# A gated transformer and Mamba kernel whose loop bodies list the same calls in another order

## The reference

```python
def attn_layer(x, Wqkv, qs, ksc, Wo):
    q, k, v = heads(x @ Wqkv)                       # 16 heads of 64
    q, k = rotary(l2norm(q) * qs), rotary(l2norm(k) * ksc)
    out = local_attention(q, k, v)                  # each window of 32 sees 64 keys
    return out @ Wo
def ffn_layer(x, g, bln, W1, b1, W2, b2):
    a, gate = split((layernorm(x) * g + bln) @ W1 + b1)
    return a * gelu(gate) @ W2 + b2
for i in range(6):
    x = attn_layer(shift_tokens(x), ...) + x
    x = ffn_layer(shift_tokens(x), ...) + x
# Mamba: conv -> silu -> delta, B, C;  h_t = exp(delta A) h_{t-1} + delta B x;  y = sum_n h C
x = x + s * silu(g)
```

## Time and profile before

| what | value |
|---|---|
| runs (3) | 1778.52 us median, 1778.05 to 1781.15 |
| profiled execution: span, first to last instruction | 1776.2 us |
| profiled execution: own time | not listed apart from its span; the runs' median is 2.3 us above the span |
| busy, share of the span | PE 95%, DVE 88%, POOL 80%, ACT 71% |
| granted TensorE clock | 0.992 in the mean; 1.00 from 100 to 1700 us |
| chain that ended last | PE 61%, DVE 15%, POOL 10%, "issue" 8% |

### The profile page before, as it was taken

The page is one execution under the profiler, slowest core; times in us unless marked ns, Lnnn a source line. Parts: engine busy times, 40 slices in busy tenths (PEclk is TensorE's granted clock), DMA queues, the critical chain, the costliest instruction groups (busy, mean ns, idle before and its releaser), DMA issues.

```text
span 1776.2 us, 73872 instructions
## 1 busy us (share of the span) xinstructions
PE 1688.0 (95%) x30944; PEld 981.9 (55%) x30944; DVE 1556.0 (88%) x2724; ACT 1253.0 (71%) x2325; POOL 1426.1 (80%) x1264
## 2 busy tenths in 40 slices
PE   3789999999999999999999999999999999999986
PEld 1355555555555555555555555555555555555552
DVE  5768999889989899889998899988998989988976
ACT  3566686767876777767778668677687677776764
POOL 1667888987889887988879888898788888788872
PEclk9899999999999999999999999999999999999998
DMA  3013233141312422133321313314131242212340
GB/s 113 22 40 71 51 84 81 40 95 41 82 40 53 106 66 55 30 71 80 82 65 34 79 43 86 84 37 93 42 84 38 53 107 65 55 31 57 75 94 24
DMA packets 94054, 113.13 MB, mean 64 GB/s; under 512 B 42318, under 2 KB 59484, under 8 KB 93724
## 3 DMA queue, kind: packets, MB, share of 16 engines
q1 hardware_dynamic: 93724, 108.41, 25.9%
HBM read 19.22 MB, written 1.05 MB: 11 GB/s over the span
## 4 chain that ended last, share of the span: by engine, by line
PE 61%; DVE 15%; POOL 10%; issue 8%; ACT 3%; SPq 1%; DMA 1%; POOLq 0%; DVEq 0%; ACTq 0%
PE bank L630 12%; PE bank L714 8%; PE bank L655 8%; PE bank L646 6%; PE bank L731 6%; PE bank L675 5%; PE bank L692 4%; DVE qn L1321 3%; PE bank L759 3%; DVE qc L1321 3%; POOL AB L1609 2%; POOL AB L1598 2%; POOL hb L1643 2%; DVE ssq L1328 2%; PE bank L774 2%
## 5 line engine op out<-in xcount | busy, mean ns | idle before, releaser
L1598 POOL TENSOR_TENSOR AB<-qc,qn 128x512 f32<-128x512 f32 x384 | 486.9, 1273 | 105.4 <-DVE qn L1321 103.3
L1609 POOL TENSOR_TENSOR AB<-AB,rinv 128x512 f32<-128x512 f32 x384 | 411.5, 1095 | 34.7 <-DVE rinv L1344 34.7
L630 PE MATMUL bank<-wqkv,XT 128*128 128x512 f32 x768 | 382.2, 600 | 4.6 <-DVE qn L1321 4.5
L1616 POOL TENSOR_TENSOR Pb<-Pb,p_rden 128x512 f32<-128x512 f32 x192 | 200.4, 1044 | 134.4 <-DVE p_rden L1365 132.1
L1004 ACT ACTIVATE qkT<-bank 128x512 f32<-128x512 f32 x384 | 228.9, 596 | 109.3 <-PE bank L655 107.6
L995 ACT ACTIVATE sq<-bank 128x512 f32<-128x512 f32 x384 | 228.4, 595 | 96.1 <-PE bank L630 96.0
L1328 DVE TENSOR_REDUCE ssq<-sq 128x8 f32<-128x512 f32 x384 | 258.4, 673 | 10.2 <-ACT sq L995 9.5
L1321 DVE TENSOR_TENSOR qc<-bank,rt 128x512 f32<-128x512 f32 x384 | 258.6, 673 | 8.8 <-ACT sq L995 5.9
L1321 DVE TENSOR_TENSOR qn<-bank,rt 128x512 f32<-128x512 f32 x384 | 261.5, 681 | 0.0
L714 PEld LDWEIGHTS bank<-PT,V 64*64 64x64 f32 x12288 | 197.0, 134 | 95.3 <-issue 89.2
L655 PE MATMUL bank<-ident,AB 128*128 128x128 f32 x1536 | 243.1, 281 | 4.5 <-ACT qkT L1004 3.3
(11 more groups left out here) (145 smaller groups left out, 2523.0 us busy)
## 6 DMA issues: line engine op xcount, KB each, us to landing
V<-V SPq DMA_DIRECT2D x672, 64.0 KB
rep<-du SPq DMA_DIRECT2D x64, 512.0 KB, 4.7
wqkv<-in_Wqkv SPq DMA_DIRECT2D x36, 256.0 KB, 3.4
XV<-XT SPq DMA_DIRECT2D x96, 64.0 KB, 2.2
wo<-in_Wo SPq DMA_DIRECT2D x6, 512.0 KB, 5.4
BC<-BC SPq DMA_DIRECT2D x8, 256.0 KB
w<-in_W SPq DMA_DIRECT2D x6, 341.0 KB, 4.5
BC<-BC SPq DMA_DIRECT2D x8, 128.0 KB
```

Of the source, the lines that this page charges most:

```text
L630: pe.matmul(R[u % 2][:], XT[:, s % NB, (u % 2) * P:(u % 2 + 1) * P], wqkv[:, (u // 2) * 512:(u // 2 + 1) * 512], start=True, stop=True).th ...
L1598: pool.tensor_tensor(AB[:, n % NAB, :], qc[:, u % 2, :], qn[:, u % 2, :], ALU.add).then_inc(rs_done, 1)
L1609: pool.tensor_tensor(o, o, r, ALU.mult).then_inc(nm_done, 1)
```

## The change

Nothing is added or removed: every engine issues the same instructions. Each loop body is permuted, and calls are moved over the loop's edge: PE's body now begins with `z_x` and ends with `turn(i + 1, 2)`, `qk(i + 2, 1)`; DVE's and POOL's bodies run one step later against their index (`rotate(i, 1)` where `rotate(i + 1, 1)` stood), with a longer tail. `T_ORDER` and `X_ORDER` follow; `M_ORDER` stays as it is. Lines in the changed kernel are 3 lower on PE and 13 lower on DVE.

```diff
-T_ORDER = [("turn", 0, 0, 1), ("turn", 1, 0, 1), ("turn", 2, 0, 1), ("turn", 3, 0, 1), ("turn_p", 0, 0, 1),
+T_ORDER = [("turn", 3, 0, 1), ("turn_p", 0, 0, 1), ("turn", 4, 0, 1), ("turn", 5, 0, 1),
...
@@ SP, loop body
-                next_qk(i + 1, 0)
-                replicate(i - 3, 2)
...
-                replicate(i - 2, 0)
-                replicate(i - 6, 7)
-                spread(i, 2)
...
+                replicate(i - 1, 0)
+                replicate(i - 3, 3)
+                spread(i + 1, 0)
+                spread(i + 1, 1)
+                next_v(i + 1, 0)
+                next_qk(i + 1, 3)
+                replicate_bc(i - 2, 1)
+                next_qk(i + 1, 1)
...
@@ PE, loop body, second half
-                w_gate(i - 3, 0)
                 turn(i, 6)
+                w_gate(i - 3, 1)
                 values_out(i, 1)
                 turn(i, 7)
-                w_gate(i - 3, 1)
-                w_out(i - 2, 3)
+                w_gate(i - 3, 2)
+                mean_x(i - 2)
+                scores(i, 3)
                 qk(i + 1, 7)
-                w_gate(i - 3, 2)
-                scores(i, 3)
                 turn_p(i, 2)
-                mean_x(i - 2)
                 value(i + 1, 0)
+                w_down(i - 3)
+                var_x(i - 2)
+                z_sum(i - 8, 2)
                 z_sum(i - 6, 1)
-                w_down(i - 3)
-                z_sum(i - 7, 2)
                 z_sum(i - 8, 3)
-                var_x(i - 2)
                 values_out(i, 2)
                 turn_p(i, 3)
                 value(i + 1, 1)
+                value(i + 1, 2)
+                turn(i + 1, 0)
+                values_out(i, 3)
+                turn(i + 1, 1)
+                value(i + 1, 3)
+                scores(i + 1, 0)
+                qk(i + 2, 0)
+                turn(i + 1, 2)
+                qk(i + 2, 1)
...
@@ POOL, loop body
+                normalise(i - 1, 3)
+                z_bu(i - 5, 4)
+                z_delta(i - 3)
```

More of the change, by code:

```diff
@@ L1476, in _ @@
             for i in STEADY:
+                sum_p(i - 1, 0)
+                sum_squares(i, 0)
+                rotate(i, 1)
+                z_scan(i - 7, 8)
+                sum_squares(i, 1)
+                z_conv(i + 1)
+                softmax(i - 1, 1)
+                rotate(i, 2)
+                z_scan(i - 9, 14)
+                sum_squares(i, 2)
+                rotate(i, 3)
+                z_scan(i - 7, 9)
+                z_scan(i - 5, 3)
+                sum_p(i - 1, 1)
+                rotate(i, 4)
@@ new lines, in _ @@
+                sum_squares(i, 3)
+                z_scan(i - 6, 5)
+                z_state(i - 10)
+                z_scan(i - 9, 15)
+                sum_squares(i, 4)
+                softmax(i - 1, 2)
+                gate(i - 4, 0)
+                rotate(i, 5)
+                res_attention(i - 3)
+                sum_squares(i, 5)
+                gate(i - 4, 1)
+                sum_p(i - 1, 2)
+                rotate(i, 6)
+                gate(i - 4, 2)
+                center(i - 3)
@@ L1477, in _ @@
+                softmax(i - 1, 3)
+                sum_squares(i, 6)
+                sum_squares(i, 7)
+                sum_p(i - 1, 3)
+                guard_q(i)
+                z_scan(i - 4, 0)
+                z_scan(i - 8, 11)
+                rotate(i, 7)
                 z_gate(i - 9)
+                norm_q(i)
+                z_scan(i - 8, 12)
+                z_scan(i - 4, 1)
+                z_scan(i - 6, 6)
                 res_ff(i - 4)
+                z_scan(i - 4, 2)
+                z_scan(i - 6, 7)
@@ L1505, in _ @@
-                sum_p(i, 2)
-                gate(i - 3, 1)
-                rotate(i + 1, 6)
-                gate(i - 3, 2)
-                res_attention(i - 2)
-                z_scan(i - 7, 11)
-                sum_squares(i + 1, 6)
-                softmax(i, 3)
-                center(i - 2)
-                sum_squares(i + 1, 7)
-                guard_q(i + 1)
-                sum_p(i, 3)
-                z_scan(i - 3, 0)
-                rotate(i + 1, 7)
-                norm_q(i + 1)
@@ L1520, in _ @@
[L1520 to L1528 removed]
+            sum_p(LAST - 1, 0)
+            sum_squares(LAST, 0)
+            rotate(LAST, 1)
+            sum_squares(LAST, 1)
+            softmax(LAST - 1, 1)
+            rotate(LAST, 2)
+            sum_squares(LAST, 2)
@@ new lines, in _ @@
+            rotate(LAST, 3)
+            z_scan(LAST_B, 3)
+            sum_p(LAST - 1, 1)
+            rotate(LAST, 4)
+            sum_squares(LAST, 3)
+            sum_squares(LAST, 4)
+            softmax(LAST - 1, 2)
+            rotate(LAST, 5)
+            res_attention(LAST - 3)
+            sum_squares(LAST, 5)
+            sum_p(LAST - 1, 2)
+            rotate(LAST, 6)
+            center(LAST - 3)
+            softmax(LAST - 1, 3)
+            sum_squares(LAST, 6)
+            sum_squares(LAST, 7)
@@ L1530, in _ @@
+            sum_p(LAST - 1, 3)
+            guard_q(LAST)
+            rotate(LAST, 7)
+            norm_q(LAST)
+            z_scan(LAST_B, 4)
+            norm_x(LAST - 3)
             softmax(LAST, 0)
```

314 lines of the change are left out of this document (140 added, 174 removed).

## The result

The changed kernel takes 1790.11 us (median of 4 runs, 1789.11 to 1791.54) against 1778.28 for the kernel before in the same comparison: ratio 1.0061 [1.0049, 1.0074]. It is slower by 12 us; the forecast was 1769.7 us, and faster.

What follows compares the result with a forecast made beforehand. PE bounds the kernel, at 95% of the span. Terms 5.7 - 8.7 + 6.0 - 4.8 - 8 + 1 = -8.8 us take 1776.2 to 1767.4; with 2.3 outside the span, 1769.7 us. Forecast's own range 1763 to 1775, overall 1758 to 1783.

Steps and rivals of the forecast that it cites:

- (e): Small waits in PE's body: two thirds of 12 us gone, -8 us, bounds -12 and +10; gaps without releaser stay.
- (a): PE's changes between full and small tiles, with products paying 0.10 us and transposes 0.056 for coming back: +5.7 us.
- the rival of one price: Products behind small tiles pay 0.056 us like transposes: tile changes cost -0.9 us, time 1763 us; chance 0.14.
- (b): PE's wait before `var_x` on steps i = 4 mod 6 goes: 8 x 1.09 = -8.7 us.
- (d): PE's third `w_gate` no longer waits for DVE's `gate`: 22 steps x 0.22 = -4.8 us.
- (c): Last `turn_p` on steps i = 4 mod 6: a stall of 0.5 to 1.0 us returns on 8 steps, +6.0 us.
- (f): The T bank: `turn_p` 0 and `turn` 4 too close on a third of the steps, +2 less 1: +1 us.
- V late: V copies queue behind `replicate(i - 1, 0)` in SP's list; 3 us of wait on 8 steps, +24: 1794 us; chance 0.10.
- the signs named beforehand: Forecast wrong if PE's body idle exceeds 30 us, `values_out` waits for a DMA, or `turn` 0 waits every step.

## Why turn 0 waits

The end of step 17 in the changed kernel, the chain from `guard_q` to `turn` 0:

```profile
684.50 0.14 DVE L1322 TENSOR_SCALAR ssc<-ssq 128x64 f32<-128x64 f32 x1
...
684.66 1.04 POOL L1632 TENSOR_TENSOR Pb<-Pb,p_rden 128x512 f32<-128x512 f32 x1 [2.47 <-DVE p_rden L1352]
...
685.66 1.27 POOL L1659 TENSOR_TENSOR hb<-rep,BC 128x512 f32<-128x512 f32 x1
685.75 1.26 DVE L1328 TENSOR_TENSOR tq<-ssc,yq 128x64 f32<-128x64 f32 x1
...
687.05 0.22 DVE L1331 SCALAR_TENSOR_TENSOR rinv<-tq,yq 128x64 f32<-128x64 f32 x1
687.35 4.05 POOL L1625 TENSOR_TENSOR AB<-AB,rinv 128x512 f32<-128x512 f32 x4 [0.42 <-DVE rinv L1331]
688.54 0.63 PE L652 MATMUL bank<-ident,AB 128*128 128x128 f32 x4 [0.34 <-POOL AB L1625]
```

A multiply of 64 columns takes 1.26 us, and it ends 0.08 us after POOL's Mamba operation, begun 0.09 us before it, has ended. On the other steps it takes 0.21. This happens in front of the `turn` 0 that ends the steps i = 4, 5 and 0 mod 6, at 22 of the 48 places. The kernel before has the same thing one instruction later and on fewer steps, which I could have read there (the same place in the program):

```profile
684.44 1.34 POOL L1643 TENSOR_TENSOR hb<-rep,BC 128x512 f32<-128x512 f32 x1
684.45 0.21 DVE L1341 TENSOR_TENSOR tq<-ssc,yq 128x64 f32<-128x64 f32 x1
684.69 1.17 DVE L1344 SCALAR_TENSOR_TENSOR rinv<-tq,yq 128x64 f32<-128x64 f32 x1
```

Grouped by line, mean ns last: the multiply went from 215 to 689 ns, its successor from 364 to 225; in sum 48 x 0.335 = 16 us more on DVE, most of it in front of `turn` 0. First the changed kernel:

```profile
L1328 DVE TENSOR_TENSOR tq<-ssc,yq 128x64 f32<-128x64 f32 x48 | 33.1, 689 | 0.2 <-ACT yq L1037 0.2
...
L1331 DVE SCALAR_TENSOR_TENSOR rinv<-tq,yq 128x64 f32<-128x64 f32 x48 | 10.8, 225 | 1.7
```

The Trainium skill has the rule, "SBUF — State Buffer", section "Who interferes with whom": a DVE instruction with two inputs in SBUF contends with a GpSimd instruction that reads SBUF, one in a mode that uses two ports with any GpSimd instruction; the port pair is held for a whole instruction, and the one that comes second is blocked until the first is done. The trace agrees: 1.26 us for 0.21.

**Four POOL operations moved behind normalise 1.** In POOL's list, from between `normalise_p(i - 1, 3)` and `normalise(i, 0)`:

```diff
                 normalise_p(i - 1, 3)
-                z_hc(i - 5, 3)
-                z_bu(i - 6, 7)
-                z_bu(i - 7, 10)
-                z_bu(i - 8, 15)
                 normalise(i, 0)
                 normalise(i, 1)
+                z_hc(i - 5, 3)
+                ...
```

> The changed kernel, with the four Mamba operations that POOL's list has between normalise_p 3 and normalise 0 moved behind normalise 1; nothing else. In the changed kernel the first small multiply of norm_q on DVE takes 1.26 us instead of 0.21 on three of six steps, each time beside one of these POOL operations that began 0.09 us before it and ends with it. Theory L (DVE is held off as long as POOL's operation lasts, and this is what turn 0 waits for): the multiply takes 0.21 us on every step, turn 0 stops waiting (9.3 us in the sum before), 1781 us, ratio about 1.0015. Rival (turn 0 waits for the chain of rotate and normalise as such, DVE's length is a mark of its record): 1790, ratio 1.0065.

Measured: 1793.41 us, ratio 1.0087 [1.0072, 1.0101]. The multiply takes 0.21 us on 47 of the 48 steps and `turn` 0's 9.3 us are gone, but the total missed: `z_delta` comes 1.2 us later, and the transfers that were late already are later still.

```profile
PE bank L627 <- DMA wqkv<-in_Wqkv: 10.6, 7, 2.9
PE bank L711 <- DMA V<-V: 6.1, 7, 1.5
```

**The same four ahead of normalise_p 3, in the kernel with early transfers.**

> The kernel with weights and V early in the transfer queue's list (1776.1 us), and besides the same four POOL operations moved the other way, ahead of normalise_p 3, where POOL stood idle for 2.4 to 3.8 us on the three kinds of step concerned. Theory L: the multiply of norm_q takes 0.21 us, turn 0 stops waiting, 1776.1 - 9.4 = 1767 us, ratio 0.994; on the fourth kind of step (i = 1 mod 6) normalise_p 3 comes 1.27 us later, which its turn_p may feel by 0.3 at most. Rival: 1776 or more, since normalise_p 3 comes later too.

Measured: 1783.35 us, ratio 1.0034 [1.0022, 1.0047], a miss to the slow side. `turn` 0 no longer waits (9.4 to 0.9), but `value` 1 does (2.6 to 11.9). On i = 1 mod 6:

```profile
537.31 1.32 POOL L1670 TENSOR_TENSOR hb<-hb,BC 128x512 f32<-128x512 f32 x1
...
538.41 2.49 DVE L1322 TENSOR_SCALAR ssc<-ssq 128x64 f32<-128x64 f32 x1
538.54 1.31 POOL L1659 TENSOR_TENSOR hb<-rep,BC 128x512 f32<-128x512 f32 x1
...
539.76 1.09 POOL L1632 TENSOR_TENSOR Pb<-Pb,p_rden 128x512 f32<-128x512 f32 x1
```

Now `guard_q` is the one that is caught. It begins inside one POOL operation and ends, at 540.90, only after the third of a row without a break. So the fourth operation, `z_bu(i - 8, 15)`, must stay where it was.

**Three of them.** The changed kernel, and the kernel with early transfers:

> The changed kernel with three POOL operations (z_hc(i - 5, 3), z_bu(i - 6, 7), z_bu(i - 7, 10)) ahead of normalise_p(i - 1, 3), where POOL was idle; the fourth, z_bu(i - 8, 15), stays. Theory L: no DVE instruction of the norm_q chain runs beside a POOL operation any more, its multiply takes 0.21 us, turn 0 stops waiting (9.3 us before) and guard_q stays short, since the fourth operation is not in its way: 1781 us, ratio 1.0015. Rival (the slack is taken by the next wait whatever one does): 1787 to 1793, ratio 1.005 to 1.009, as when the four were moved behind normalise 1.

> The same three POOL operations ahead of normalise_p 3, in the kernel with weights and V early in the transfer queue's list (1776.1 us). Theory L: 1776.1 - 8.5 = 1767.6 us, ratio 0.994. With the fourth operation moved too it was 1783.4, because guard_q stood beside two POOL operations on i = 1 mod 6 and took 2.49 us; without it that wait of value 1 (1.83 us on each such step) must be gone. Rival: 1776 or more.

Measured: 1785.26 us, ratio 1.0033 [1.0019, 1.0047], and 1769.90 us (1766.09 to 1771.33), ratio 0.9942 [0.9927, 0.9958]. The gains are 4.8 and 6.2 us where 9 and 8.5 were expected; by the ratios, each against the kernel before in its own rounds, they are 5.0 and 8.9. The direction and the trace are the theory's (`guard_q` 285 ns, the multiply 234 in the mean, no wait of `turn` 0 or for a DMA). The body of the second:

```profile
100.00:1700.00 1600.00, 1580.12 (x29545) 930.79 (x29548) 1441.63 (x2521) 1165.32 (x2181) 1352.71 (x1188) 1.00 0.27 63
```

PE is idle 19.9 us there. This version beats both kernels.

**guard_q by another instruction.** Two edits of that version, one of PE's list and one of ACT's and DVE's, made it much slower (below): in each `guard_q` had moved into POOL's work. In the one with `turn(i + 1, 2)` first (1805.33 us) it took 2.95 us on i = 1 mod 6. The sums of squares now stand in pairs with 1e-24, which is written once at the start:

```diff
-                dve.tensor_scalar(ssc[:], ssq[:], 1e-24, None, ALU.max).then_inc(ssc_done, 1)
+                dve.reduce_max(ssc[:], ssq[:], AX_X).then_inc(ssc_done, 1)
```

> The kernel of the run before (transfers, three POOL operations, turn 2 first; 1805.3 us, where guard_q took 2.95 us beside two POOL operations on i = 1 mod 6), with guard_q computed another way: the sums of squares stand beside a constant 1e-24 and a tensor_reduce takes the larger of each pair, in place of the tensor_scalar with max. The result is the same. In the traces so far no tensor_reduce of DVE was ever longer beside POOL's work, so theory L expects guard_q at about 0.2 us on all steps and the waits of value 1 and value 2 on i = 1 and 4 mod 6 gone: 1767.6 us, ratio 0.993 to 0.995. Rival (DVE is simply late there and the length in the record is something it would have waited for anyway): 1800 or more, ratio over 1.012.

Measured: 1778.51 us, ratio 1.0000 [0.9986, 1.0015]: 27 us from one small instruction, with no call moved in the loops. `guard_q` of the kernel with the `tensor_scalar`, then of the one with the `tensor_reduce`:

```profile
L1322 DVE TENSOR_SCALAR ssc<-ssq 128x64 f32<-128x64 f32 x48 | 33.2, 691 | 0.0
```

```profile
L1324 DVE TENSOR_REDUCE ssc<-ssq 128x64 f32<-128x128 f32 x48 | 11.3, 235 | 0.0
```

That the length is a cause and not a mark is shown by this run. Part of the 27 us is the clock. In the body of the kernel at 1805.33 us seven stretches, 24 us in all, are at its lower level, four of them behind a wait of `value` 1 of 2.3 us; in this one three, 10 us in all. By starts that is 12 us against 5. One of the four:

```profile
762.39 2.62 PE L643 MATMUL bank<-wqkv,XV 128*128 128x512 f32 x4 [2.34 <-DVE qn L1308]
...
763.61:767.02 3.41, 3.41 (x54) 0.50 0.24 58
```

The expected 1767.6 was missed by 10.9 us. Of these 5 are the three stretches that are left, each behind waits of 1.1 and 0.5 us on i = 4 mod 6, and 2.4 are `values_out` 2, which waits 0.3 us more on each of these steps than in the best version. What the rest is isn't shown, and no run has the `tensor_reduce` in the best version itself.

## The price of coming back into the full array

In the changed kernel `qk` behind `scores` takes 0.96 us from start to start (621.21 to 622.17) and the one without a change before or behind it 0.86 (622.61 to 623.47), as at the end of the kernel before:

```profile
621.21 1.13 PE L627 MATMUL bank<-wqkv,XT 128*128 128x512 f32 x2
622.17 0.60 PE L652 MATMUL bank<-ident,AB 128*128 128x128 f32 x4
622.61 1.02 PE L627 MATMUL bank<-wqkv,XT 128*128 128x512 f32 x2
623.47 1.03 PE L789 MATMUL bank<-HT,inW 128*128 128x256 f32 x4
```

**The other way round in the kernel before.** Four `qk` put behind small tiles; one of the four swaps:

```diff
                 scores(i, 0)
-                turn(i, 2)
                 qk(i + 1, 0)
+                turn(i, 2)
```

> The kernel before with four swaps on PE alone: behind scores 0, 1, 2 and values_out 0 the qk goes ahead of the transposes. The number of changes between full and small tiles stays what it is. If a product pays 0.10 us for coming back from small tiles where transposes pay 0.056, each swap costs 0.044 to 0.05 us: 4 x 48 x 0.047 = +9 us, 1787 us, plus or minus what the waits change (the turn and turn_p get 0.86 us more time). If each change has one price, 1778 us.

Measured: 1825.90 us, ratio 1.0269 [1.0255, 1.0282]. The bare sum grew by 8.1 us, near the price's 9; the total is another matter. One of the four swaps had left two `turn` side by side, and ACT's copy-out of T cost 20 us:

```profile
PE bank L655 <- ACT qkT L1004: 20.5, 29, 1.2
```

**The transposes first in the changed kernel.** The `qk` behind `scores(i, 3)` and `scores(i + 1, 0)` change places with `turn_p(i, 2)` and `turn(i + 1, 2)`.

> The changed kernel with two swaps on PE alone: turn(i + 1, 2) right behind scores(i + 1, 0), and turn_p(i, 2) right behind scores(i, 3), where a qk stood behind the small tiles in both; the qk follows. The number of changes between full and small tiles is the same. If coming back costs a product of 512 columns 0.104 and four transposes 0.056, this is 2 x 48 x 0.047 = -4.5 us in the bare sum of PE: 1785.6 us against the changed kernel's 1790.1, ratio 1.004, unless the transposes, 0.86 us earlier, have to wait for rotate or normalise_p. If each change has one price, as the rival of the prediction had it: 1790, ratio 1.0065, and the bare prices of the units the same in both places.

Measured: 1804.66 us, ratio 1.0155 [1.0137, 1.0173]. The bare sum fell by 3.9 us, but `turn_p` 2, asked for 0.86 us sooner, waits for `normalise_p`: 29 waits of a `turn_p` for POOL, 15.1 us in all, where the changed kernel has 10, 5.4 us. With early transfers as well it was 1792.64, where 1771.5 was expected if the terms add and 1776 to 1779 if the transposes wait.

**turn 2 first, in the best version.**

> The kernel with weights and V early and the three POOL operations moved (1769.9 us), and on PE turn(i + 1, 2) right behind scores(i + 1, 0), the qk behind it. If the price of coming back into the full array is 0.104 us for a product and 0.056 for four transposes, and normalise 2 is now done in time: 48 x 0.047 = 2.3 us less, 1767.6 us, ratio 0.993. If turn 2, 0.86 us earlier, has to wait for normalise 2, up to 2 to 6 us come back: 1770 to 1774, with waits named for POOL at the transposes.

Measured: 1805.33 us, ratio 1.0153 [1.014, 1.0167]; the bare sum fell by 1.9. Of the rest, `value` 1 behind the blocked `guard_q` waits 21.5 us where it waited 2.6, and 12 are the lower clock. So the price of 0.10 against 0.056 us is seen in every trace and in no total: each swap that saved it lost more.

## The stall on i = 4 mod 6

The changed kernel at step 16, where the earlier trace rows showed the wait of `var_x`:

```profile
645.10 0.89 PE L672 MATMUL bank<-qkT 64*32 64x64 f32 x64
645.92 1.13 PE L627 MATMUL bank<-wqkv,XT 128*128 128x512 f32 x2
...
648.18 1.02 PE L741 MATMUL bank<-sqx,mean 128*128 128x512 f32 x2
649.93 1.14 PE L711 MATMUL bank<-PT,V 64*64 64x32 f32 x64 [0.73 <-ACT PT L1009]
651.53 0.63 PE L689 MATMUL bank<-ident,Pb 128*128 128x128 f32 x4 [0.46 <-POOL Pb L1632]
```

`var_x` starts at once behind `value`; then `values_out` 2 waits for `copy_p`, which ACT's list has behind `expo` 3, and `turn_p` 3 waits as forecast: 0.76 + 0.53 us on 8 steps.

**copy_p ahead of expo 3**, on ACT, in the changed kernel.

> The changed kernel with one call moved in ACT's list: copy_p(i, 2) ahead of expo(i, 3). In the changed kernel, where i = 4 mod 6, values_out 2 starts 0.8 us late because copy_p 2 stands behind expo 3, which waits for softmax 3. Theory D: 8 x 0.8 us is an upper bound, and since the last turn_p of these steps is late anyway, most of it comes back as its wait: -1 to -6 us, 1784 to 1789. Rival E says that this chain is the main loss: -8 us or more, 1782 or less.

Measured: 1796.62 us, ratio 1.0109 [1.0087, 1.0131], a miss for both. `values_out` 2 waits 1.2 us in place of 6.1, and `turn_p` 3 13.2 in place of 5.3: `expo` 3 is later for all steps. In this trace, of a run of 1792.7 us, the waits are 1.6 us longer in sum; what makes the median 4 us longer than that run isn't shown.

**copy_p behind expo 3 but ahead of copy_v, and sum_p ahead of sum_squares 7**, in the best version.

> The kernel of the run before, with two swaps more: on ACT copy_p(i, 2) ahead of copy_v(i + 1, 0) (still behind expo 3), on DVE sum_p(i - 1, 3) ahead of sum_squares(i, 7). In the trace copy_v takes 0.58 us at a time when copy_p's input is long there, and sum_squares 7 0.6 us when expo 3 has ended. On i = 4 mod 6 values_out 2 should start 0.5 us sooner (0.76 to 0.28 of wait) and normalise_p 3 0.5 us sooner: 8 x 0.5 to 0.6 = 4 to 5 us, 1763 us, ratio 0.9915. Rival (what is gained there, turn 0 or value 1 loses, as with the other swap of copy_p): 1768 or more.

Measured: 1812.44 us, ratio 1.0184 [1.017, 1.0198]. `values_out` 2 waits less (6.1 to 2.4), but `guard_q`, now behind `sum_p` and so beside `normalise_p` on nearly every step, takes 798 ns in the mean for 285, and `value` 1 waits 27.5 us. With `turn` 2 first as well it was 1824.23, where 1761 was expected. Early transfers, `turn` 2 first and the four operations behind `normalise` 1, all in the changed kernel, gave 1801.22, where 1764.5 was expected: the swap of `turn` 2 is in both.

## Why the prediction was wrong

The forecast was 20.4 us too low. The step that failed is the sum itself in two places: it had no term for the transfers of the weights, and it took the chain of `turn` 0 in (e) as just fitting. By its own steps, with what each measured:

- (a) +5.7 forecast, +5.1 in the bare sum. Right, and the rival of one price is refuted.
- (b) -8.7: gone, 8.7. (d) -4.8: gone, 4.8. Right.
- (c) +6.0: mis-sized. The stall was there, and on the same steps, but with `copy_p` in front: +5.2 before `values_out` 2, and before `turn_p` 3 another 4.1 on these steps (+2.3 over all kinds of step).
- (e) The step that failed within the sum. I had reckoned `norm_q` at 0.3 us from the earlier trace rows and the chain of `turn` 0 as just fitting. The multiply takes 1.26 us on three of six steps because of what POOL's new list has beside it; +7.0 before `turn` 0, where a part of -8 was booked. The bound of +10 that I named for it was nearly met.
- (e) again: the gaps without releaser that I let stay went (10.5 to 2), which no term had. It hides half of the other errors. Why they go is not shown: in the version with the old transfer list two came back. `qk` 0 behind `scores` 0 loses 1.1 us in the changed kernel, 5.0 with the old transfer list, 2.4 and 3.3 with early transfers, all with one list of PE. So a gap of this kind is not a fixed cost of the instructions, as (e) had it.
- (f) +1: `turn` 4 starts at its bare distance on all steps, and what stands before `turn` 5 grows by 0.7 us in sum. The 0.06 us for a weight load that no longer hides shows in no run.
- V late: the rival was right in kind; its price in the changed kernel is 2 to 3 us and not 24. `z_delta` ended 13.3 us behind `qk` 7, as reckoned; V was up to 1.0 us late on three steps of eight.
- Not in the sum at all: the layer's weights. I followed SP's list for V, and did not ask when `next_qk` 1 and 2 are issued and wanted: -11.6 us when they are issued earlier. This is the largest error of the forecast.
- Of the signs named beforehand two came: PE's idle in the body is over 30 us, and `values_out` waits for a DMA. `turn` 0 waits on 21 of 44 steps, not on every one.

The two causes shown to matter, late transfers (11.6 + 2.4) and the blocked multiply (6.2), make 20.2 us as measured one after the other, and the version without them runs in 1769.9 us. That this is the forecast's number is in part luck: the vanished gaps (8.5 us, no term of mine) stand against stalls on the steps of (c) and waits of (e) that were to be smaller.

## What to carry to other kernels

When an order changes, walk every queue that issues transfers and write down, for each one, when it is issued and when it is first wanted; the largest new wait here was for a transfer that never showed up in the waits before. When DVE and POOL lists move against each other, look at the durations of small DVE instructions, not only at their order: one that is several times its usual length beside a POOL row is a blocked one. In the kernel where `guard_q` was blocked, doing it as a `tensor_reduce` gave back 27 us; it takes 0.235 us where the unblocked `tensor_scalar` takes 0.14. And a wait of PE can cost more than its length: look at the granted clock of the stretch behind it.

## What the runs showed of the hardware that I had not expected

A blocked DVE instruction can stay blocked over several POOL operations that follow without a break: `guard_q`, 0.14 us alone, took 2.49 and 2.95 us, each to the end of the third POOL operation. It isn't so everywhere. On other steps it ended 0.05 us after the first of two such operations, as here in the changed kernel, where the second had begun before the first ended:

```profile
611.72 1.26 POOL L1614 TENSOR_TENSOR AB<-qc,qn 128x512 f32<-128x512 f32 x1
...
612.02 1.01 DVE L1322 TENSOR_SCALAR ssc<-ssq 128x64 f32<-128x64 f32 x1
...
612.95 1.04 POOL L1632 TENSOR_TENSOR Pb<-Pb,p_rden 128x512 f32<-128x512 f32 x1
```

What decides between the two isn't shown. Blocked by one operation with a pause of POOL behind it, the multiply took 1.26 us. `guard_q` as a `tensor_reduce` was never longer than 0.29 us. And coming back from small tiles costs a 512-column float32 product 0.10 us, four transposes 0.056.
